# A convolution tap moved from ScalarE to VectorE, and a rounding from VectorE to GpSimd, in a transformer layer with quantised feed-forward

## The reference

```
g  = gelu(x @ K.T)                     # K: 4096 x 1024
x  = layernorm(x + (g / |g|_2 * sqrt(4096)) @ V)
q  = act_quant(x)                      # per token, 8 bits: round(x * 127 / max|x|), scaled back
h  = q @ weight_quant(w1).T            # w1: 4096 x 1024, weights become -1, 0, 1 times a mean
h  = silu(depthwise_conv1d(h, 3 taps, along the tokens) + b)
x  = layernorm(x + act_quant(h) @ weight_quant(w2).T)
```

## Time and profile before

| | us |
|---|---|
| median of the runs (2) | 4284.36 |
| lowest, highest | 4270.96, 4297.77 |
| profiled execution | 4299.36 |
| its span, slowest core (core 3) | 4297.8 |
| spans of the other cores | 4229.9 to 4280.1 |
| first stage, to the first window's loads | about 1917 |
| VectorE busy, whole span | 2077.2 (48%) |
| TensorE matmul busy | 2562.3 (60%) |
| ScalarE busy | 1344.6 (31%) |
| GpSimd busy | 853.4 (20%) |

### The profile page before, as it was taken

The page is one execution under the profiler, slowest core; times in us unless marked ns, Lnnn a source line. Parts: engine busy times, 40 slices in busy tenths (PEclk is TensorE's granted clock), DMA queues, the critical chain, the costliest instruction groups (busy, mean ns, idle before and its releaser), DMA issues.

```text
span 4297.8 us, 50851 instructions; the slowest of 8 cores (4229.9 to 4297.8 us)
## 1 busy us (share of the span) xinstructions
PE 2562.3 (60%) x14308; PEld 1449.4 (34%) x14308; DVE 2077.2 (48%) x3999; ACT 1344.6 (31%) x2222; POOL 853.4 (20%) x1073
## 2 busy tenths in 40 slices
PE   3477767878777777763455635554545445554544
PEld 2244334444444444432222322232323222322322
DVE  2355445555555555522544445445444454445445
ACT  0111111111111111113444544454445444544453
POOL 2111100000000000002322323232223322332232
PEclk9677777777888888876677767777777777776767
DMA  6732222122222222123000000000000000000000
GB/s 102 164 93 91 84 74 64 46 64 64 66 67 72 77 70 69 55 68 125 6 25 25 1 25 25 25 1 25 25 15 10 25 25 10 15 25 25 6 15 35
DMA packets 174230, 204.77 MB, mean 48 GB/s; under 512 B 111456, under 2 KB 127872, under 8 KB 172928
## 3 DMA queue, kind: packets, MB, share of 16 engines
q1 hardware_dynamic: 144752, 117.61, 8.9%
q0 software_dynamic: 29200, 83.90, 7.6%
HBM read 159.52 MB, written 58.74 MB: 51 GB/s over the span
## 4 chain that ended last, share of the span: by engine, by line
DVE 31%; PE 26%; ACT 17%; DMA 10%; issue 9%; another core or an unknown queue 2%; POOL 2%; DVEq 2%; ACTq 1%; POOLq 0%; SPq 0%
PE pA L560 12%; ACT ca L786 6%; PE pB L498 6%; DVE mg L823 5%; DVE ca L798 5%; DVE htr L780 4%; ACT i32tr L898 4%; ACT hq_sb L902 3%; DMA wtmp<-w 3%; ACT hc_buf L819 3%; DVE hc_buf L895 2%; DMA kbt<-k 2%; DVEq L90 2%; PE pC L484 1%
## 5 line engine op out<-in xcount | busy, mean ns | idle before, releaser
L769 PE MATMUL pB<-yqTw,W1T 128*128 128x258 bf16 x2816 | 480.3, 331 | 488.0 <-DVE htr L780 484.7
L498 PE MATMUL pB<-xT_sb,KT 128*128 128x256 bf16 x4096 | 616.0, 302 | 48.8 <-ACT g_sb L507 47.8
L805 POOL TENSOR_TENSOR hc_buf<-ca 128x256 f32<-128x256 f32 x512 | 371.3, 725 | 1135.7 <-DVE ca L798 1106.2
L798 DVE SCALAR_TENSOR_TENSOR ca<-htr,cwb_sb,ca 128x256 f32<-128x256 f32 x512 | 248.2, 485 | 621.1 <-ACT ca L786 621.1
L769 PEld LDWEIGHTS pB<-yqTw,W1T 128*128 128x128 bf16 x2816 | 307.8, 115 | 658.7 <-issue 573.5
L560 PE MATMUL pA<-V_sb,g_sb 128*128 128x512 bf16 x2048 | 515.3, 421 | 0.0
L498 PEld LDWEIGHTS pB<-xT_sb,KT 128*128 128x128 bf16 x4096 | 401.9, 106 | 175.3 <-issue 69.8
L250 POOL DMA_DIRECT2D wtmp<-w x256 | 137.6, 538 | 1574.2 <-DVE wqb L315 1179.8
L890 POOL TENSOR_TENSOR hc_buf<-hc_buf,S_sb 128x512 f32<-128x512 f32 x256 | 323.8, 1265 | 622.5 <-DVE S_sb L872 587.8
L786 ACT ACTIVATE ca<-htr,cwb_sb 128x256 f32<-128x256 f32 x512 | 306.7, 599 | 423.9 <-DVE htr L780 418.4
L507 ACT ACTIVATE g_sb<-pB 128x256 bf16<-128x256 f32 x512 | 195.0, 384 | 755.1 <-PE pB L498 749.2
(11 more groups left out here) (117 smaller groups left out, 2476.0 us busy)
## 6 DMA issues: line engine op xcount, KB each, us to landing
wtmp<-w POOLq DMA_DIRECT2D x256, 256.0 KB, 3.1
x_sb<-x SPq DMA_DIRECT2D x16, 1024.0 KB, 7.7
y_sc<-y_sb SPq DMA_DIRECT2D x16, 1024.0 KB, 5.0
y_win<-y_sc SPq DMA_DIRECT2D x32, 512.0 KB, 3.3
out<-y_win SPq DMA_DIRECT2D x32, 512.0 KB, 2.6
kbt<-k POOLq DMA_DIRECT2D x32, 256.0 KB, 3.9
V_sb<-v POOLq DMA_DIRECT2D x1, 8192.0 KB, 57.2
yqT_sc<-yqT_sb SPq DMA_DIRECT2D x32, 256.0 KB, 2.6
```

The lines of the kernel that those rows point to most:

```text
L498: O("tensor", lambda t, ss=ss, j=j, lo=lo, hi=hi: t.matmul(pB[:, lo:hi], KT[:, j * S + 128 * ss: j * S + 128 * (ss + 1)], xT_sb[:, j * TA: ...
L769: r = t.matmul(mp[:, lo:hi], W1T[:, j * H + 128 * hc: j * H + 128 * (hc + 1)], yqTw[wb][:, j * (TW + 2):(j + 1) * (TW + 2)], start=(j == 0 ...
L798: O("vector", lambda v, hc=hc, hb=hb: v.scalar_tensor_tensor(ca[hc % 2][:], htr[hb][:, 1:TW + 1], cwb_sb[:, 4 * hc + 1:4 * hc + 2], ca[hc ...
L805: O("gpsimd", lambda g, hc=hc: g.tensor_tensor(hc_buf[:, hc * TW:(hc + 1) * TW], ca[hc % 2][:], ca3[hc % 2][:], ALU.add), W(c2_ok, c3_ok, ...
```

## The change

In `emit_conv_chunk` tap 2 (`ca3`) is computed by VectorE's `tensor_scalar` instead of a ScalarE activation. It stands in VectorE's queue between the scaling into `htr` (L780) and the sum (L798). The next writer of the same `htr` buffer waits, of ScalarE, for the first tap alone. The waits on `sc.cur("ve")` at the sum now include the new instruction. In `emit_quant_pair` the rounding in place of L895 is issued by GpSimd, behind the multiply of the same pair, and the first ScalarE instruction waits for GpSimd instead of VectorE. Sizes, types and the values computed are as before.

```diff
--- before.py
+++ after.py
@@ -789,12 +789,12 @@
             bias=cwb_sb[:, 4 * hc + 3:4 * hc + 4]),
             W(htr_ok, cwb_ok, lastB[f"ca{hc % 2}"]), "ac")
         c1_ok = sc.cur("ac")
-        O("scalar", lambda s, hc=hc, hb=hb: s.activation(
-            ca3[hc % 2][:], htr[hb][:, 2:TW + 2], AF.Identity,
-            scale=cwb_sb[:, 4 * hc + 2:4 * hc + 3], bias=0.0),
-            W(lastB[f"ca3{hc % 2}"], sc.cur("ac")), "ac")
-        lastB[f"htr{hb}ac"] = sc.cur("ac")
-        c3_ok = sc.cur("ac")
+        lastB[f"htr{hb}ac"] = c1_ok
+        O("vector", lambda v, hc=hc, hb=hb: v.tensor_scalar(
+            ca3[hc % 2][:], htr[hb][:, 2:TW + 2],
+            cwb_sb[:, 4 * hc + 2:4 * hc + 3], None, ALU.mult),
+            W(lastB[f"ca3{hc % 2}"], sc.cur("ve")), "ve")
+        c3_ok = sc.cur("ve")
         O("vector", lambda v, hc=hc, hb=hb: v.scalar_tensor_tensor(
             ca[hc % 2][:], htr[hb][:, 1:TW + 1],
             cwb_sb[:, 4 * hc + 1:4 * hc + 2], ca[hc % 2][:],
@@ -892,12 +892,12 @@
             hc_buf[:, sl].rearrange("q (c t) -> q c t", c=2),
             s2b, ALU.mult),
             W(s2_ok, dbg_ok if p == 0 else None, sc.cur("gp")), "gp")
-        O("vector", lambda v, sl=sl: v.tensor_scalar(
+        O("gpsimd", lambda g, sl=sl: g.tensor_scalar(
             hc_buf[:, sl], hc_buf[:, sl], MAGIC, MAGIC, ALU.add, ALU.subtract),
-            W(sc.cur("gp"), sc.cur("ve")), "ve")
+            W(sc.cur("gp")), "gp")
         O("scalar", lambda s, sl=sl: s.activation(
             i32tr[:], hc_buf[:, sl], AF.Identity, bias=cqc[:]),
-            W(consts_ok, sc.cur("ve"), sc.cur("ac")), "ac")
+            W(consts_ok, sc.cur("gp"), sc.cur("ac")), "ac")
         hc_last[2 * p] = hc_last[2 * p + 1] = sc.cur("ac")
         O("scalar", lambda s, sl=sl: s.activation(
             hq_sb[:, sl], i32tr[:], AF.Identity, bias=m256c[:]),
```

## The result

The changed kernel takes 4552.1 us (median of 11 runs, 4523.8 to 4626.8) against 4267.9 us (median of 10, 4258.8 to 4328.0): ratio 1.065, 95% interval 1.060 to 1.071. That is some 280 us slower, far outside the forecast of 4213 to 4360. Some executions of either kernel run with the cores of one die at a lower granted clock and take some per cent longer; the ratio leaves the clearly slow ones out.

The account below looks back on a forecast made before the run. Engines waiting for each other in a ring were taken as the bound. Fifteen windows at -2.30 us (-34.5) and the last at +7.8 gave -27 us, moving the 4284.4 us median to 4258, range 4213 to 4360.

Parts of the forecast that it names:

- P: GpSimd's time for one quantisation pair, multiply plus rounding: forecast 2.205 us where it cost 1.41.
- B: Quantisation of pairs 0 to 7 in each of 15 windows: 19.11 us against 15.94, +3.17.
- C: Quantisation of pairs 8 to 11 in each of 15 windows: 10.29 us against 9.43, +0.86.
- The last window: Sixteen quantisation pairs in a row at the end: 36.8 us against 29.05, +7.8.
- D: Quantisation of pairs 12 to 15, rounding no longer queued behind VectorE's maximum: ScalarE's next tap 6.33 us earlier per window.
- Part one: Moving tap 2 from ScalarE to VectorE in convolution chunks: fits VectorE's 0.93 us idle before the sum, worth nothing.
- GpSimd is slow at this: Rival, chance 0.11: the rounding on GpSimd takes 1.265 us, in all +94 us, 4378.
- The clock rival: Rival, chance 0.05: TensorE's second product behind D runs at the lower clock, +84 us, 4342.
- D was freed: Rival, chance 0.04, denied this: GpSimd work beside the maximum stretches it, D gives 0, sum +68 us, 4352.
- The tap did not overflow: Rival, chance 0.06, said it would: tap 0.2 us over its gap in 512 chunks, +102 us, 4360.

Follow-up runs that it names:

- the two-element rounding: The changed kernel with the GpSimd rounding instruction cut to 2 of its 512 elements; ratio 0.975 against the kernel before.
- the roundings first: The kernel before, with the VectorE roundings of pairs 12 to 15 queued ahead of the maximum, nothing moved to another engine; ratio 0.987.

## Why the prediction was wrong

**The step that failed is the size of one term, X**, the duration of the rounding on GpSimd: 0.65 us was put in, 1.92 measured. Its upper bound was wrong too. I held the two-input instruction of the same size, 1.265 us, for a ceiling, because one input should not cost more than two. That is no bound: the one-input instruction turned out dearer than the two-input one, with one operation (1.49 us) as with two. And the 292 ns row is that of a select by index; the sum carried the 0.84 ns per element worked out from it over to an arithmetic instruction that takes 3.35. One kind of instruction said nothing of another, although the engine, the type and the number of inputs were the same.

**The rest of the sum held.** With X = 1.923, P is 3.478. B: 8P + 1.47 = 29.3, measured 29.4. C: 4P + 1.47 = 15.4, measured 15.42. The last window: 57.2, measured 57.7. D: beyond X = 1.27 GpSimd decides, as the step said; 15.4, measured 15.45. Fifteen windows and the last give +262 us, against the 266 of the stretches and the 271 of the table.

**Part one was right.** The tap fits behind GpSimd's add: it ends 0.15 us behind it where up to 0.29 had been allowed, and 0.38 us before the sum is due, where the margin was put at 0.01 to 0.17 (the 0.17 leaves out the 0.10 us between VectorE instructions that the 0.01 has in it; alike, they are 0.01 and 0.07).

**D was right as a mechanism**, and it is the only gain in the change: 6.3 us a window was there to be had (the two-element rounding shows 12.83 for 12.77), and 3.7 were left with the long instruction.

**The rivals.** "GpSimd is slow at this" was the true one, with 0.11, and it was priced at +94 us because its price was taken from the same false ceiling. The rule in the Trainium skill (GPSIMD Engine Reference, § 4.1 Engine selection) that elementwise work belongs on VectorE speaks for this outcome, though its factor of about two on VectorE's 426 ns would be an estimate of only 0.85 us, and not the 1.265 that the prediction matched it with. Its exception for one-input work as roughly line-rate and the 1.03 cycles per element of § 3.1, which the prediction set beside its own 0.65, do not hold for this instruction: 1923 ns for 512 elements is an estimate of 4 cycles per element, by that page's 1.2 GHz, once the 0.21 us are off, and 3 with a single operation. The clock rival did not come: behind stretch D the second product runs at a granted clock of 1.00 in the changed kernel (2343.3 to 2348.9 us) and also in the one with the two-element rounding (2250.2 to 2255.8), where D takes 12.83 us. The maximum was stretched by 0.13 us only (7.14 for 7.01), and D was freed as far as X let it. The tap did not overflow.

## What to carry to other kernels

An instruction that no row of the trace shows on its new engine is the widest term of a sum, and a row of another operation does not bound it from above: price it with a ceiling well over the dearest neighbour, or measure it by itself first. In a ring of engines, ask for each stretch who is the limit; the same move can gain where it lies under a long instruction and lose five times that where it becomes the limit (3.7 us in D against 19.5 in B and C). And before moving an instruction to another engine, look whether it only stands in the wrong place in its queue: four roundings set ahead of one maximum gained 5.0 us a window where the same four moved to GpSimd gained 3.6.

## What the runs showed of the hardware

- GpSimd's `tensor_scalar` in float32, 128 partitions, SBUF to SBUF: 0.21 us fixed, plus 2.50 ns per element with one operation and 3.35 ns with two. Its `tensor_tensor` costs 2.11 ns per element. For 512 elements: 1491, 1932 (1923 in the changed kernel) and 1265 ns; for two elements with two operations 223 ns. VectorE takes 426 ns at best for the same 512 elements and two operations.
- VectorE and GpSimd hold each other up, but not in every pairing. Behind GpSimd's two-input instructions VectorE's tap waits: it takes 352 ns with nothing beside it, 445 in the median, mostly behind an add, and 1.40 us when it began 0.02 us into a multiply:

```profile
2771.01 1.27 POOL L890 TENSOR_TENSOR hc_buf<-hc_buf,S_sb 128x512 f32<-128x512 f32 x1
2771.03 1.40 DVE L793 TENSOR_SCALAR ca<-htr,cwb_sb 128x256 f32<-128x256 f32 x1
```

  In the other direction, a GpSimd rounding that began 0.06 us behind a tap took 2.08 instead of 1.92 us (one case in the changed kernel). But a tap that begins inside a GpSimd rounding hardly waits: in stretch D above it starts at 2331.98, with 1.01 us of the rounding left, and takes 0.35 us; of the 28 taps of that trace that began inside a rounding none took over 0.46. Section "Who interferes with whom" of the Trainium skill's page SBUF — State Buffer describes a lock that the first one holds for its whole instruction; the trace agrees for GpSimd's multiply and add and not for its rounding, and there the measurement decides.
- The maximum over 16 chunks is stretched by little more than 0.1 us when GpSimd works beside it: in stretch D it takes 7.01 us before and mostly 7.12 to 7.15 us in the changed kernel. Part of that is not GpSimd's: with the roundings first, where GpSimd has finished and ScalarE's conversions run beside it, it is 7.08.
